# A graph network on one core: the attention's message pass with its weights and one-hot numbers in PSUM, and two banks for each sum

## The reference, cut to what matters

```python
h = (x @ W.T).reshape(n, 8, 64)
h_src = h[src]                                    # one row of 512 per edge
e = leaky_relu(e_src + e_dst, 0.2) * (1 + et_emb[edge_type]) * edge_weight[:, None]
e_max = zeros((n, 8)).at[dst].max(e)
e = exp(e - e_max[dst])
e_sum = zeros((n, 8)).at[dst].add(e)
alpha = e / (e_sum[dst] + 1e-10)
msg = h_src * alpha[:, :, None]
out = zeros((n, 8, 64)).at[dst].add(msg).reshape(n, 512)
out = layernorm(out + x) * ln_gamma + ln_beta
```

## Time and profile before

| what | us |
|---|---|
| median of three runs | 2324.63 (2314.41 to 2325.7) |
| the profiled execution's own time | 2326.27 |
| its span, first to last instruction | 2324.5 |
| first and last issue of a gather in the message pass (start) | 1415.0 and 1679.5 |
| all issues of a gather, summed (line 657, 176 of them) | 212.2 |
| DVE's `multiply`, summed (line 676, 88 of them) | 107.8 |

### The profile page before, as it was taken

How to read it: one execution, slowest core, us unless ns; L and a number is a source line. 1 busy time by engine, 2 the same in 40 slices (tenths; PEclk the granted TensorE clock), 3 DMA queues, 4 the chain that set the end, 5 groups by cost and what they waited for, 6 DMA issues and landing times. The chain is left out here.

```text
span 2324.5 us, 31922 instructions
## 1 busy us (share of the span) xinstructions
PE 1787.4 (77%) x8445; PEld 1136.6 (49%) x8446; DVE 1328.8 (57%) x3171; ACT 459.1 (20%) x847; POOL 515.7 (22%) x460
## 2 busy tenths in 40 slices
PE   0676967886775789999864855777748879899988
PEld 0343855653334445555443743444424635584567
DVE  7455667767764237777659877777775721111112
ACT  0111300113333115555421330000011011001100
POOL 0000000000001017666136005788740100200000
PEclk9887558998997899999975557999979989999989
DMA  0997008980009317667400014666600500430034
GB/s 17 207 215 157 0 0 190 204 183 2 0 12 365 111 66 210 195 186 180 72 37 1 0 36 110 175 173 172 166 0 10 158 0 0 161 119 0 0 122 149
DMA packets 70315, 241.89 MB, mean 104 GB/s; under 512 B 11552, under 2 KB 24977, under 8 KB 62571
## 3 DMA queue, kind: packets, MB, share of 16 engines
q1 hardware_dynamic: 36234, 135.73, 20.8%
q0 software_dynamic: 30944, 101.16, 16.3%
q10 hardware_dynamic: 3072, 4.20, 0.9%
HBM read 209.39 MB, written 31.66 MB: 104 GB/s over the span
## 5 line engine op out<-in xcount | busy, mean ns | idle before, releaser
L1309 PE MATMUL n_pY<-weights,n_xT_block 128*128 128x512 f32 x640 | 284.9, 602 | 0.0
L657 POOL DMA_INDIRECT e_rows<-tab_h,idx_h x176 | 212.2, 1206 | 206.9 <-ACTq L639 153.6
L1398 PE MATMUL e_pA<-parts,e_number 128*128 128x512 f32 x1000 | 233.9, 397 | 31.0 <-DMA e_number<-tab_edges_from 20.7
L702 PE MATMUL e_pS<-e_rows,e_onehot_ring 128*128 128x512 f32 x352 | 196.0, 645 | 70.4 <-issue 40.6
L1398 PEld LDWEIGHTS e_pA<-parts,e_number 128*128 128x128 f32 x1000 | 191.1, 192 | 73.6 <-DMA e_number<-tab_edges_from 20.9
L880 POOL DMA_INDIRECT e_rows<-tab_q,idx_q x192 | 182.1, 948 | 177.1 <-DVE e_onehot_bf L889 100.3
L1309 PEld LDWEIGHTS n_pY<-weights,n_xT_block 128*128 128x128 f32 x640 | 121.7, 194 | 142.4 <-issue 142.4
L953 PE MATMUL e_pS<-e_rows,e_onehot_f 128*128 128x512 f32 x384 | 180.9, 595 | 0.0
L1940 POOL DMA_DIRECT2D a_in<-in_L_gnn_a_src x1 | 1.0, 988 | 748.6 <-issue 748.6
L767 PE MATMUL count_pA<-count_onehot_d,count_onehot_s 128*128 128x512 f16 (+1 forms) x576 | 117.0, 352 | 50.2 <-DVE count_onehot_d L746 41.4
L676 DVE TENSOR_TENSOR e_rows<-e_rows,edge_weights 128x1024 f32<-128x1024 f32 x88 | 107.8, 1225 | 72.4 <-DMA e_rows<-tab_h,idx_h 72.3
(11 more groups left out here) (327 smaller groups left out, 3040.9 us busy)
## 6 DMA issues: line engine op xcount, KB each, us to landing
basis_piece<-in_L_gnn_basis SPq DMA_DIRECT2D x128, 480.0 KB, 12.2
e_number<-tab_edges_from SPq DMA_DIRECT2D x20, 1280.0 KB, 5.5
tab_edges_from<-counts_turned SPq DMA_DIRECT2D x10, 1280.0 KB, 6.9
tab_edges_to<-counts_total SPq DMA_DIRECT2D x10, 640.0 KB, 4.6
e_number<-tab_edges_to SPq DMA_DIRECT2D x10, 640.0 KB, 4.4
tab_w<-basis_wout ACTq DMA_DIRECT2D x128, 32.0 KB
weights<-tab_w SPq DMA_DIRECT2D x4, 1024.0 KB
w_raw<-in_L_gnn_W SPq DMA_DIRECT2D x3, 1024.0 KB, 8.8
```

Source lines behind the costliest of these rows:

```text
L657: pool.indirect_dma_start(rows[:, q, s, :], None, table, bass.IndirectOffsetOnAxis(idx[:, j * 2 + s:j * 2 + s + 1], 0)).then_inc(got[q], 16)
L702: nc.tensor.matmul(pS[:, u % 4, :], ohr[:, u % 4, s, :], rows[:, u, s, :], start=s == 0, stop=s == 1)
L1309: ins = nc.tensor.matmul(py[:, k, w, :], xt[:, k, c, :], weights[:, c, :], start=c == 0, stop=c == 3)
L1398: ins = nc.tensor.matmul(pA[:, b % 4, :], number[:, b % 2, k, :], parts[k // NB][n][:, k % NB, :], start=k == 0 and n == 0, stop=k == K - ...
```

## The change

The weights and the numbers 0 to 127 are copied to three banks of PSUM when the stage begins (four copies on DVE), and `build` and `multiply` read them there. To make room, `pS` and `pN` have two banks each instead of four, pair j uses bank j modulo 2, and PE waits for the sums of pair j-2 to be taken instead of those of pair j-4. DVE's order for step j becomes build j, accumulate j-2, multiply j. The copy of the weights that PE reads (line 704) stays in SBUF.

```diff
-        pS, pN = ps("pS", [P, 4, D], F32), ps("pN", [P, 4, D], F32)
+        pS, pN = ps("pS", [P, 2, D], F32), ps("pN", [P, 2, D], F32)
+
+        PER = D // H
+        BANKS = -(-SLOTS // PER)
+        pW = ps("pW", [P, BANKS, PER, H], F32)
+        assert SLOTS * H + P <= BANKS * D
+        pI = pW[:, BANKS - 1, SLOTS - (BANKS - 1) * PER:PER, :].rearrange("p s h -> p (s h)")[:, 0:P]
...
+        in_psum = sem("in_psum")
...
             nc.vector.memset(side[:, :, :], 0.0).then_inc(zeroed, 1)
+            for k in range(BANKS):
+                n = min(PER, SLOTS - k * PER)
+                nc.vector.tensor_copy(pW[:, k, 0:n, :], weight[:, k * PER:k * PER + n, 0:H]).then_inc(in_psum, 1)
+            nc.vector.tensor_copy(pI, C.f("iota_p")).then_inc(in_psum, 1)
             v.wait_ge(zeroed, 2)
+            v.wait_ge(in_psum, BANKS + 1)
...
-                    ohr[:, u % 4, :, :], C.f("iota_p").unsqueeze(1).to_broadcast([P, 2, P]),
+                    ohr[:, u % 4, :, :], pI.unsqueeze(1).to_broadcast([P, 2, P]),
...
-                    r, r, weight[:, bass.ds(i * 16 + u * 2, 2), 0:H].unsqueeze(3).to_broadcast([P, 2, H, DH]),
+                    r, r, pW[:, :, :, :].rearrange("p k s h -> p (k s) h")[:, bass.ds(i * 16 + u * 2, 2), :]
+                    .unsqueeze(3).to_broadcast([P, 2, H, DH]),
...
-                nc.vector.tensor_tensor(a, pS[:, u % 4, :], a, ALU.add).then_inc(added, 1)
+                nc.vector.tensor_tensor(a, pS[:, u % 2, :], a, ALU.add).then_inc(added, 1)
...
-                nc.vector.tensor_tensor(a, pN[:, u % 4, 0:ns], a, ALU.add).then_inc(nadded, 1)
-
-            lagged(v, NSTEP, BODYP, [(0, build), (0, multiply), (2, accumulate)], last=1)
+                nc.vector.tensor_tensor(a, pN[:, u % 2, 0:ns], a, ALU.add).then_inc(nadded, 1)
+
+            lagged(v, NSTEP, BODYP, [(0, build), (2, accumulate), (0, multiply)], last=1)
...
-                wait(pe, nadded, j - 3)
-                wait(pe, added, j - 3)
+                wait(pe, nadded, j - 1)
+                wait(pe, added, j - 1)
                 for s in range(2):
-                    nc.tensor.matmul(pS[:, u % 4, :], ohr[:, u % 4, s, :], rows[:, u, s, :],
+                    nc.tensor.matmul(pS[:, u % 2, :], ohr[:, u % 4, s, :], rows[:, u, s, :],
...
-                        pN[:, u % 4, 0:ns], ohr[:, u % 4, s, :],
+                        pN[:, u % 2, 0:ns], ohr[:, u % 4, s, :],
```

## The result

The changed kernel takes 2283.14 us (median of 6 runs, 2276.91 to 2285.68), the kernel before beside it 2326.18. The ratio is 0.9832, 95% interval 0.9809 to 0.9854. The profiled execution has a span of 2283.8 us and took 2285.68, 40.6 less than that of before. All of it lies in the message pass. Its first issue starts at 1415.0 us in both profiles, from there to the last sum it is 233.9 us instead of 275.1, and from there to the end 634.9 instead of 634.4.

The account below looks back on a forecast made before the run. The message pass was taken to run at POOL's pace, 265.5 us for 176 issues. The profiled 2326.3 - 45.7 + 1.0 = 2281.6; with the median of runs 1.6 lower, 2280 us was predicted, range 2272 to 2297.

Parts of the forecast that it names:

- POOL: Message pass: all 176 gather issues cost the undisturbed 0.946 us, 166.5 us instead of 212.2, a gain of 45.7 us.
- Rival 2: Message pass: POOL isn't freed, issues still wait, 3.02 us per pair stays; 2325 us, chance 0.07.
- VectorE's step: DVE's time per pair in the message pass: 2.19 us, under POOL's 2.49, so DVE still waits for rows.
- My upper end of 2.45: Most that DVE's pair was said to take, in us, with the step from build at 0.63.
- Rival 3: Multiply in the message pass slows down through its repeated weight read from PSUM; at twice its length 2360 us, chance 0.04.
- Banks and order: Two banks and accumulate before multiply: PE's new wait costs 0, with 0.3 us to spare for the reverse wait.
- The beginning: Start of the message pass: four copies of 2.2 us in all; 1.0 us counted on the path, ends 0 and 2.2.
- The end: End of the message pass: 10.6 us from last issue to last sum, left unchanged.
- Rival 1: Message pass: VectorE takes the lead, a pair takes 2.55 to 2.65 us; 2290 us at 2.60, chance 0.14.
- e0: Another stage that gathers, used as comparison: its add has one input in PSUM, and an issue under it takes 0.94 us.

Follow-up runs that it names:

- chip B: Chip of one follow-up batch: kernel before 2320.50 us, changed kernel 2278.85 us, ratio 0.9816.
- spread rows: Changed kernel, but empty places gather different rows instead of row 0: message pass only 2276.95 us (0.9805); both gathering stages, on another chip, 2355.51 us (0.9994).
- A and C: Chips of the two other follow-up batches: kernel before 2356.53 and 2359.07 us; no variant there had a ratio under 0.9978.

## Why the prediction was right

*POOL.* The step held: forecast 166.5 us for the issues, measured 166.5; last start near 1635, measured 1633.9. That VectorE's second SBUF input is the cause of the long issues is shown by the series of variants, whose issues sum to 212 to 216 us with all 88 multiplies in SBUF, 186 to 191 with 44, 169 to 173 with none but the builds, and 166.5 to 166.9 with neither. The 45.7 us are 0.52 us for each of 88 pairs, and 44 x 0.52 us above 166.5 is 189.4. That the time follows the issues rests on POOL's pace, which is the stage's pace in both profiles, and on the four kernels with free or nearly free issues on chip B; no kernel with held issues but the one before was timed there. Rival 2 (POOL isn't freed) is refuted.

*VectorE's step.* Forecast 2.19 us, found 2.15 to 2.25 from multiply to multiply less the wait for rows; idle before the multiply 21.9 us where I had 26. My upper end of 2.45 left out the 0.1 us for reading PSUM that the same paragraph names. With it the end was 2.55, over POOL's 2.49, so that only rival 1 was costed for it. Rival 3 (the repeated read from PSUM is slow) is refuted by 1216 ns. The table of the Trainium skill that gives a PSUM read 62 cycles more (VectorE: DVE Perf Modes, section on the TRN2 errata) is not borne out: the build takes 418 ns from PSUM and 416 from SBUF.

*Banks and order.* Costed at nothing. Alone they brought 0.9992 and 0.9978, and the old order with two banks 1 us on chip B, so nothing beyond a few us either way.

*The beginning.* I took 1.0 us for copies that hold up POOL; it was 0, the issues beside them are 0.94 and 0.95 us long.

*The end* is the term that I sized wrong: "10.6 us, which I leave" became 15.0. The last pairs have no edges in them and gather row 0 again and again. Their multiplies start 3.45 us apart in the changed kernel (1622.77 to 1643.47 in six steps) and 3.5 us before (1664.53 to 1685.56): the gathers set this pace in both. Against the usual pair of 2.49 and 3.02 us that is 6 x 0.96 = 5.8 us lost instead of 2.9, and two passes of PE at the lower clock level behind its waits (1.96 and 1.84 us instead of 1.10) add 1.6. So some 4.4 us of the 45.7 went there, which makes the gain of the stage 41.2 us instead of 44.7 (45.7 less the 1.0 for the copies) and the forecast 3 us too good (2280 for 2283.14). That is within the range.

*Rival 1* (VectorE takes the lead) was refuted where the change was timed and on chip B, and is what happens on C. I had looked for it in the length of instructions; it came through stalls that no row of before showed. That the change was timed on a chip without them was luck: nothing in the forecast allowed for them, and on chip C the whole change with the spread rows was worth nothing.

What stays open is what stalls VectorE on A and C. Four things are known of the message pass:

- The stalls stand in front of accumulate. It begins with a read of the block number into a register, but that read is not what takes the time: it takes 0.30 us, once 0.58, and in all 20 cases of the change with spread rows it had ended before the stall began.
- They keep to the loop. In that run twelve of them are the accumulates 19, 27, 35, 43 and 22, 30, 38, 46, then 52, 60, 68, 76, and three more are 57, 65, 73: each time eight pairs apart, which is one turn of the loop. Something that VectorE needs once a turn, such as its next instructions, is a rival that no run tested.
- The four kernels there whose issues were freed in part or in full had 15 to 22 stalls of 48 to 51 us in this stage. The four whose multiplies all read SBUF had 3, 0, 2 and 7, of 14.7, 0, 14.5 and 42.8 us. So the gain may be lost not only through little room but also through more stalls; one trace of each does not show why.
- The changed kernel without the spread rows was not timed on A or C; for these chips I rely on the multiply alone (A) and on the change with spread rows (C).

## What to carry to other kernels

When GpSimd issues the DMAs that pace a stage, compare its issues with those in a stage where VectorE reads PSUM: the longer ones name the VectorE instruction with two inputs in SBUF, and moving one of them to PSUM frees the issue; here it cost nothing in length (1216 ns for 1225). Then look at what the new pace meets next, above all at the end (padding that gathers a single row) and at how much room is left to the engines that had been waiting. A gain that leaves 0.3 us of slack per step was there on two chips and gone on two where VectorE stalled. And read a wait that the profile puts down to an engine against that engine's own rows: here over half of it was none.

## What the runs showed of the hardware

- A gather of 128 times the same row of 2 KB ran at 141 GB/s with a DMA share of 1.01, different rows at 211 GB/s with 0.75; landing took up to 7.6 us where the change was timed and 5.9 on chip B, and 3.8 at most with different rows on chip B.
- What holds an issue acts at its beginning. The one that starts 0.72 us before a multiply from SBUF is not held. One that starts 0.40 us into such a multiply takes 1.63 us and ends 0.82 us after it. In the run with every second multiply in PSUM all 39 issues over 1.05 us started 0.05 to 0.92 us into a multiply from SBUF and ended 0.81 to 0.83 us after it; with the multiply alone in PSUM all 26 such issues started 0.04 to 0.18 us into a build and ended 0.81 to 0.83 us after that.
- The multiply is not lengthened by an issue that is under way: the one of 1543.32 us starts 0.22 us before the issue of 1542.60 ends, and takes its 1.23 us.
- On chips A and C VectorE had stalls of 0.7 to 12.6 us for which the profile shows no cause. In e0, whose loop has the same code in all kernels, first to last issue took 286.0 to 287.3 us there and 257.9 to 258.7 us on the other two chips. That is some 28 to 29 of the 36 to 39 us by which the kernel before was slower there than on B.
